# An earlier front in a tuned language-model tower: embedding product in another PSUM place, next step's front two units ahead, output addition ahead of the cell exchange

## What is computed

```
h = tok_ref(x, ...)                       # table row per id, joined with STFT features of the sequence
h = h + attn_ref(layernorm(h), ...)       # 8 heads; 64 summary tokens, 17-wide windows, summary rows of 7
h = h + ffn_ref(layernorm(h), ...)        # top 2 of 8 LSTM experts
...
gates = xt @ Wi + h @ Wh + b              # per expert; 512 rows a choice, two choices
c = sigmoid(f_) * c + sigmoid(i_) * tanh(g_)
h = sigmoid(o_) * tanh(c)                 # output h @ Wo + bo, weighted by the router
```

## Time and profile before

| | |
|---|---|
| median of 3 runs | 1681.88 us (1679.94 to 1682.21) |
| profiled execution, its own time | 1681.96 us |
| span of its trace | 1680.2 us |
| PE busy (matmul) | 94% |
| DVE busy | 91% |
| ACT busy | 53% |
| DMA queue of SP, share of 16 engines | 45.5% |

### The profile page before, as it was taken

The page is one execution under the profiler, slowest core; times in us unless marked ns, Lnnn a source line. Parts: engine busy times, 40 slices in busy tenths (PEclk is TensorE's granted clock), DMA queues, the critical chain, the costliest instruction groups (busy, mean ns, idle before and its releaser), DMA issues.

```text
span 1680.2 us, 21553 instructions
## 1 busy us (share of the span) xinstructions
PE 1576.4 (94%) x7416; PEld 757.3 (45%) x7416; DVE 1524.8 (91%) x2440; ACT 887.0 (53%) x1004; POOL 49.5 (3%) x43
## 2 busy tenths in 40 slices
PE   7767999999999999999999999999999999999998
PEld 3433444444444444444444444444444444444443
DVE  5578999999999999999999999999999999999876
ACT  4256545454554655545465554545546555454554
POOL 1000000000000000000000000000000000000000
PEclk8898999999999999999999999999999999999999
DMA  4133535344454454545446354454534445364452
GB/s 138 22 84 109 154 115 162 124 124 145 132 155 121 140 137 130 148 120 144 136 129 159 115 162 127 120 146 133 154 120 141 136 131 150 118 149 130 151 154 66
DMA packets 254766, 219.75 MB, mean 131 GB/s; under 512 B 131429, under 2 KB 174360, under 8 KB 254657
## 3 DMA queue, kind: packets, MB, share of 16 engines
q1 hardware_dynamic: 254576, 218.36, 45.5%
q10 hardware_dynamic: 80, 0.02, 0.0%
HBM read 73.06 MB, written 4.74 MB: 46 GB/s over the span
## 4 chain that ended last, share of the span: by engine, by line
PE 52%; DVE 36%; issue 8%; ACT 2%; DMA 1%; SPq 1%; POOL 0%; DVEq 0%; ACTq 0%
PE gates L584 14%; PE gates L583 14%; PE gates L578 11%; DVE C L1094 4%; DVE tmp L1118 4%; PE yp L590 3%; DVE H L1087 3%; DVE C L1122 3%; DVE H L1101 2%; DVE tmp L1111 2%; PE FA L523 2%; DVE z L1131 2%; PE FA L508 2%; ACT tmp L747 1%; DVE pr L966 1%
## 5 line engine op out<-in xcount | busy, mean ns | idle before, releaser
L747 ACT ACTIVATE tmp<-gates,bias_sb 128x1024 f32<-128x1024 f32 x504 | 558.5, 1111 | 505.2 <-PE gates L584 489.4
L584 PE MATMUL gates<-H,wh_sb 128*128 128x512 f32 x960 | 490.2, 592 | 0.0
L583 PE MATMUL gates<-H,wh_sb 128*128 128x512 f32 x960 | 490.2, 592 | 0.0
L578 PE MATMUL gates<-xm,wi_sb 128*128 128x512 f16 x1512 | 411.5, 381 | 6.4 <-ACT tmp L747 4.4
L584 PEld LDWEIGHTS gates<-H,wh_sb 128*128 128x128 f32 x960 | 182.4, 190 | 229.6 <-issue 229.6
L578 PEld LDWEIGHTS gates<-xm,wi_sb 128*128 128x128 f16 x1512 | 143.6, 99 | 282.6 <-issue 191.6
L754 ACT ACTIVATE tmp<-C 128x1024 f32<-128x1024 f32 x128 | 135.3, 1057 | 171.0 <-DVE C L1122 167.3
L583 PEld LDWEIGHTS gates<-H,wh_sb 128*128 128x128 f32 x960 | 182.3, 190 | 69.1
L1111 DVE SCALAR_TENSOR_TENSOR tmp<-tmp 128x1024 f32<-128x1024 f32 x120 | 145.2, 1210 | 36.2 <-ACT tmp L747 35.7
L1094 DVE COPY_PREDICATED C<-masks,Cx 128x1024 f32<-128x1024 uint16 x120 | 158.6, 1321 | 1.5 <-DMA Cx<-C 1.5
L1101 DVE SCALAR_TENSOR_TENSOR H<-tmp 128x1024 f32<-128x1024 f32 x128 | 155.9, 1218 | 2.1 <-ACT tmp L754 2.1
(11 more groups left out here) (167 smaller groups left out, 1246.2 us busy)
## 6 DMA issues: line engine op xcount, KB each, us to landing
Hx<-H SPq DMA_DIRECT2D x240, 256.0 KB, 2.6
Cx<-C SPq DMA_DIRECT2D x240, 256.0 KB, 2.4
masks<-mask_scratch SPq DMA_DIRECT2D x128, 256.0 KB, 5.1
roww<-mw_scratch SPq DMA_DIRECT2D x128, 256.0 KB, 3.4
diag<-pr SPq DMA_DIRECT2D x64, 112.0 KB, 3.1
diag<-vwin SPq DMA_DIRECT2D x64, 112.0 KB, 3.1
out_dram<-h SPq DMA_DIRECT2D x16, 256.0 KB, 2.7
C<-in_wi SPq DMA_DIRECT2D x1, 2048.0 KB, 10.8
```

The lines of the kernel that those rows point to most:

```text
L578: mm(fed, wi_sb[:, e, wpart, rows_of], xm[:, e % 2, vpart, :], start=(wpart == HI and vpart == HI), stop=(first and wpart == LO))
L583: mm(fed, wh_sb[:, e, rows_of], H[:, e, 0:SEQ], start=False, stop=True)
L584: last = mm(other, wh_sb[:, e, rows_of], H[:, e, SEQ:2 * SEQ], start=True, stop=True)
L747: A(tmp[:, gate_at(gate, e), :], gates[:, (n - 1) % 2, :], ACT.Tanh, bias=bias_sb[:, e, gate:gate + 1], scale=UNSCALE).then_inc(s_tanh, 1)
```

## The change

The embedding product `emb` writes to the first half of `FA` instead of `FB`; its wait for the copies out of `maskT` moves to `xT`, the next writer of `FB`, and `emb` now waits for `attn` (the last reader of that half). Every piece of the front from `ids` to `values` and `f_part`, on all engines, stands two units earlier, `attn`, `proj`, `projT`, `moments2` and `xn2` one unit; `x2T` and what follows it up to `maskT` stay. On DVE, `add_y` goes ahead of `swap_c` in unit 7. No operation on data is added or removed. Ahead of step 0, `BUSY` now has the key 25 twice (`maskT` with 11 dummy products and `emb` of the next front with 13), and the second entry, 13, is the one that holds.

```
-    SP_AT = dict(ids=-8, qbd=1, vz=5, rows=25, wrow=28)
-    PE_AT = dict(emb=-5, xT=-2, qkv=-1, summary=2, window=4, feature=10, values=15, proj=17, projT=18, x2T=20,
+    SP_AT = dict(ids=-10, qbd=-1, vz=3, rows=25, wrow=28)
+    PE_AT = dict(emb=-7, xT=-4, qkv=-3, summary=0, window=2, feature=8, values=13, proj=16, projT=17, x2T=20,
                  logits=21, maskT=25)
...
-    EARLY = 8
+    EARLY = 10
...
                 if t == PE_AT["emb"]:
                     pe.wait_ge(S["onehot"], b1)
                     pe.wait_ge(S["enc"], 16 * b1)
                     if not is_zero(b):
-                        pe.wait_ge(S["mrow"], b)
-                        pe.wait_ge(S["wT"], b)
+                        pe.wait_ge(S["attn"], b)
                     for i in range(TILES):
-                        last = mm(FB[:, i * D:(i + 1) * D], rows[0:ENC0 + NFR, i * P:(i + 1) * P], table[:, :],
+                        last = mm(FA[:, 0, i * D:(i + 1) * D], rows[0:ENC0 + NFR, i * P:(i + 1) * P], table[:, :],
...
                 if t == PE_AT["xT"]:
                     pe.wait_ge(S["xn"], b1)
                     pe.wait_ge(S["hsb"], b1)
+                    if not is_zero(b):
+                        pe.wait_ge(S["mrow"], b)
+                        pe.wait_ge(S["wT"], b)
...
-                    A(h_sb[:, :, :].rearrange("p t d -> p (t d)"), FB[:, :], ACT.Copy).then_inc(S["hsb"], 1)
+                    A(h_sb[:, :, :].rearrange("p t d -> p (t d)"), FA[:, 0, :], ACT.Copy).then_inc(S["hsb"], 1)
...
+                    if t == YADD_AT and not first:
+                        add_y(s - 1, 1 - par)
                     if g == 3 and e < E - 1 and not first:
                         swap_c(s, e + 1)
...
-                    if t == YADD_AT and not first:
-                        add_y(s - 1, 1 - par)
                     run_front(lambda u, b: front(u, b, b % 2), t, s)
```

More of the change, by code:

```diff
@@ L53, in lm_tower_kernel @@
     Q_SCALE = 2.0 ** 4
-    SP_AT = dict(ids=-8, qbd=1, vz=5, rows=25, wrow=28)
-    PE_AT = dict(emb=-5, xT=-2, qkv=-1, summary=2, window=4, feature=10, values=15, proj=17, projT=18, x2T=20,
+    SP_AT = dict(ids=-10, qbd=-1, vz=3, rows=25, wrow=28)
+    PE_AT = dict(emb=-7, xT=-4, qkv=-3, summary=0, window=2, feature=8, values=13, proj=16, projT=17, x2T=20,
                  logits=21, maskT=25)
-    ACT_AT = dict(h=-5, xT=-2, qkv=-1, split=0, summary=4, window=7, pr_hi=11, feature=12, proj=17, x2T=20,
+    ACT_AT = dict(h=-7, xT=-4, qkv=-3, split=-2, summary=2, window=5, pr_hi=9, feature=10, proj=16, x2T=20,
                   choice=22, maskT=25)
-    DVE_AT = dict(onehot=-6, moments=-4, xn=-3, pw=0, q_lo=0, kv_lo=1, v_win=2, w_max=3, s_max=5, s_sub=6, w_sum=7,
-                  w_out=8, s_sum=9, s_norm=10, f_max=11, p_lo=12, p_T=13, f_sum=14, f_part=14, attn=15,
-                  moments2=18, xn2=19, x_lo=21, choice1=22, choice2=22, weights=23)
-    EARLY = 8
+    DVE_AT = dict(onehot=-8, moments=-6, xn=-5, pw=-2, q_lo=-2, kv_lo=-1, v_win=0, w_max=1, s_max=3, s_sub=4, w_sum=5,
+                  w_out=6, s_sum=7, s_norm=8, f_max=9, p_lo=10, p_T=11, f_sum=12, f_part=12, attn=14,
+                  moments2=17, xn2=18, x_lo=21, choice1=22, choice2=22, weights=23)
+    EARLY = 10
     MASKS_AT = 26
```

## The result

The changed kernel takes 1684.17 us (median of 20 runs, 1679.95 to 1688.2), the kernel before 1681.29 (20 runs beside it). The ratio is 1.002, with a 95% interval of 1.0013 to 1.0027. So it is slower by 0.2%, at the bound of what can be told from no change; 1666 was predicted, and the range ended at 1684.

A forecast was written before the change was run, and what follows sets the result against it. It took a step to be a chain, DVE from unit 5 to 19, PE from unit 20 to 5. Loop -8.8, tail -2.7 and start -4 gave -15.5 from 1681.96, so 1666 us, range 1650 to 1684.

The forecast's parts named there:

- PE comes to it about 2 us early and waits, which is a new wait of PE: At the embedding product in unit 25: PE waits about 2 us for onehot; the route to xT is just covered, within 0.2.
- the "slower" rival: Embedding product late in unit 25, every excess microsecond of its route costing 13 times; 1695 with 1 us beyond; chance 0.17.
- a wait of 1.5 and a cost of nothing: At unit 8's bias product: PE still waits about 1.5 us for the addition, at no cost in the loop.
- the addition "at nothing": Addition ahead of the exchange in unit 7: starts 1.19 us earlier, costed at nothing in the loop, bounds -0.4 to +0.3.
- 101.3: Step length from x2T to x2T: 97.98 + 3.13 + 0.2, which is 0.68 us less than 101.99.
- the root, which I had at nothing: DVE's 1.12 us wait at xn for GpSimd's root: gone, with 3.6 us of work put against it.
- the 0.2 of unit 4: In unit 4, DVE's hidden may wait for its tanh: 0.2 us a step, between 0 and 0.6.
- 97.98: DVE's own work in a step, in us: 101.99 - 4.01, unchanged by the edit.
- The loop should have given -8.8: Steps 0 to 13: 0.68 us less a step over 13 rounds from U to U, -8.8 us.
- ahead of step 0, -4: Start and step 0: dummy products no longer hold emb (-2.0) and DVE waits go; -4 us, between -7 and 0.
- the tail, -2.7: After the last U of unit 29: no new wait, old ones go, 1.55 + 0.60 + 0.74 - 0.2, -2.7 us.
- The reading of the 3.1 us: DVE's new wait at U of unit 29: xn, transposition, gate, tanh take 4.26, less hidden 1.13, 3.13 us; bounds 2.5 to 4.5.

The follow-up runs named there:

- fill_both: Changed kernel plus five unread PE products in each stop, ahead of the embedding product and ahead of unit 8's bias product: 1671.34 us, ratio 0.9946.
- ylate_oh23: Changed kernel, no extra products, one-hot rows moved to unit 23, bias product and first expert's product behind gate 9 instead of 8: 1669.96 us, ratio 0.9934.
- fill_emb: Changed kernel plus five unread PE products only in the stop ahead of the embedding product: 1683.6 us, ratio 1.0023.
- fill_y: Changed kernel plus five unread PE products only in the stop ahead of unit 8's bias product: 1679.22 us, ratio 0.999.
- add_alone: Kernel before with only the addition moved ahead of the exchange: 1679.08 us, ratio 0.9998.
- xm29_fill: fill_both with DVE's masked input and exchange of unit 30 done in unit 29, ahead of U: 1671.78 us, ratio 0.9946.
- ylate_oh23_xm29: ylate_oh23 with DVE's masked input and exchange of unit 30 done in unit 29: 1669.32 us, ratio 0.9929.
- route_xm29: ylate_oh23 with xT behind gate 29, q, k, v and pw a unit later, and unit 30's masked input and exchange in unit 29: 1648.29 us, ratio 0.9812.

## Why the prediction was wrong

**What failed.** The step "PE comes to it about 2 us early and waits, which is a new wait of PE" at the embedding product. I costed this stop only by whether the route behind it was covered, and it was: `xT` waits 0.36 us for `xn`, not the reverse. I did not ask what standing still does to PE's clock behind it, and in the "slower" rival the only price was the length of the route. Four runs show that this was the loss: with PE busy in both stops (`fill_both`) or both stops gone by order (`ylate_oh23`) the time is 1671.3 and 1670.0; with one stop left (`fill_emb`, `fill_y`) it is 1683.6 and 1679.2, and every fall stands behind that stop. The same price was missing at the bias product, where I had a wait of 1.5 and a cost of nothing. In the sum, -15.5 was forecast and +2.9 came (1684.17 - 1681.29), 18.4 more: 13.9 are the falls, and the rest is in the terms for the two ends of the program, below. The trace of before had stops too, up to 1.9 us, but no fall in its 13 steps, which is why nothing in it warned me.

The Trainium skill (TensorE: Matmul & The Clock Gate, A second HAM failure mode: psum-queue depth-cycling) says that short, frequent idle spots of PE between groups of matmuls can make the clock swing between its levels. The trace agrees in kind: a stop stood ahead of each of the nine falls, eight of them of 1.11 to 1.22 us and the first of 1.44.

**The second failure: the addition "at nothing".** On the kernel before that holds (0.9998). In the changed kernel its place is worth 31 us. Of these 9.6 come without any fall; I take it that PE's work from unit 8 on has become nearly as late as DVE needs it, but the rows show only 0.3 a step of it, a wait of DVE for PE's product at `h`. The rest is clock falls (nineteen in 13 steps, two of them twice as long, and not nine), more frequent behind the longer stop; behind it they reach DVE as a wait of 1.9 or 3.5. I had bounded it by rows of before, where DVE was the late one, although my own sum had PE and DVE change roles.

**What held.** A step without a fall takes 101.24 to 101.32 against 101.3. DVE's waits are 3.12 at U of unit 29 (3.13 forecast) and 0.3 at `xn` (the root, which I had at nothing; the 0.2 of unit 4 shows in some steps only). Own work is thus 101.28 - 3.1 - 0.3 = 97.9, against 97.98. The waits for `xn2`, `attn` and `kf` are gone. PE stops 1.1 at `emb` (2 forecast) and 1.22 at the bias product (1.5). The loop should have given -8.8: `ylate_oh23` has exactly that, 1316.9 against 1325.7 of before, and the changed kernel has +5.1.

**Two terms with the wrong size: ahead of step 0, -4, and the tail, -2.7.** Ahead of the loop, `x2T` comes at 224.66 instead of 229.07, which looks like the -4, but that agreement is luck. In `add_alone`, whose program is that of before up to step 1, the first `x2T` comes at 68.07 instead of 71.27 and the one at the loop's start at 223.80; the mean granted clock ahead of the first `x2T` was 0.95 there and 0.86 in the trace of before. With the change in, the loop starts anywhere from 223.35 (`fill_y`) to 230.05 (`fill_emb`). So one pair of traces can't show a gain of 4. The medians bound it: `fill_both` is 8.7 below the kernel before beside it (1671.34, 1680.07) and `ylate_oh23` 10.9 (1669.96, 1680.9), of which the loops give 8.6 and 8.8. Both ends together gained 0.1 to 2.1 us, by intervals some 2 us wide either way, and not 6.7.

In the tail, from the last `x2T` (1555.48) to the end it is 125.2 us, of before 125.4 (1680.2 - 1554.76): -0.2, and 126.3 in `ylate_oh23`: nothing was won there. In the last step PE and ACT set the time rather than DVE, as I read it: DVE's U waits 16.1 us for tanh there in the kernel before and still 14.5 in the changed one.

**The reading of the 3.1 us** was half right. Its size and its parts (`xn`, transposition, gate, tanh) were, and putting a gate ahead of the transposition removed two thirds of it. But a wait with such a source can't be filled with DVE's work, as I expected when I moved 1.8 us into it; in `xm29_fill`, `ylate_oh23_xm29` and `route_xm29` the wait came back in other places.

**What stays open.** Why stops of 1.9 us ahead of `x2T` in the kernel before and of 1.47 ahead of `xT` in `ylate_oh23` never bring the clock down, while 1.1 and 1.2 in the changed one do. So "a stop brings the clock down" is shown for two places only, and not as a rule. The stops differ in what lies around them: full gates at `x2T`, small transpositions and the small products of the embedding, or the bias product with its 8 rows, at the other two. The length of the step differs too, and with it when the stops come. No run here separates these.

Why filling the one stop made falls behind the other go from two to eleven is open too; the times under `fill_emb` give a likely reason, not tested by a run. A fall makes a step 102.5 long, nearly the 102.40 between the falls, so the next stop comes at nearly the same point before the next fall.

## What to carry to other kernels

A new or longer stop of TensorE can have two prices: what is late behind it, and products behind it at half the clock. The second was invisible in the profile of before, so on a kernel like this one, where TensorE is busy for 94% of the span and just in time, give it a chance of its own, and keep a version at hand in which the stop is filled or moved.

Where the engine that sets the pace changes with the edit, price each part against the new balance: a move that is worth nothing alone was worth 31 us in company. When waits stay the same in sum after the waiter's order is changed, suspect the route that feeds it, and try another order of the feeding engines. And before a trace's start or end is taken to confirm a small term, compare it with a run whose program is the same there: here that alone moved by 3 us.

## What was unexpected of the hardware

A stop of TensorE of 1.11 to 1.22 us was enough for its granted clock to go from 1.00 to 0.50 for 3.4 us (958.99 to 962.40, for one), within 2 us of the stop's end. Pairs of 128x512 f32 products then took up to 1.91 us instead of 1.02. One such fall cost a step 1.2 to 1.7 us. Five products of no use in the stop (1.24 us) prevented it at that place.

A stop doesn't bring a fall each time: seven of 13 steps behind the embedding product, two or eleven of 13 behind the bias product by whether the other stop was there, and none in 13 steps behind a stop of 1.9 us before `x2T` in the kernel before or one of 1.47 before `xT` in `ylate_oh23`. So the loss can't be read off from one step; the lengths of all steps, from one `x2T` to the next, showed it at once.
